# Expert phase of a fused decoder layer: gate products spread, weights loaded in chained pieces, feature transposes behind the weighted sums

## The chip, the cores and the metric

One core of a Trainium2 chip runs one program. The metric is the time of one launch on the device in microseconds (us), as the median over several runs. The profile comes from one further execution.

## The reference, cut to what matters

The input is 4096 tokens (2 sequences of 2048) of 512 features; a decoder layer of three parts is computed in float32, each with a residual.

```
x = x + gated_recurrence(layernorm(x))
x = x + cross_attention(layernorm(x), ctx) @ Wo + bo       # 16 heads, 77 keys
xf = layernorm(x)
scores = xf @ gate_W + gate_b                              # 4 experts
top2, weights = top_k(scores, 2), softmax(top2 scores)
expert e: layernorm(relu(layernorm(xf @ W1[e] + b1[e]) * g1[e] + be1[e]) @ W2[e] + b2[e]) * g2[e] + be2[e]
x = x + xf + sum over the two experts of weight * expert(xf)
```

With the reference's own inputs the first 2048 tokens send 697, 1052, 1151 and 1196 rows to experts 0 to 3.

## The kernel before, in words

**Precision.** A float32 product is made of three products of a high and a low part (TERMS). ScalarE (ACT) writes the high part of an operand, VectorE (DVE) then writes what is left as the low part; TensorE (PE) takes high*high, high*low, low*high.

**Phase A and B.** Eight chunks of 512 tokens pass the recurrence (A) and then the attention (B). A turn of B interleaves the attention of chunk c with the output projection, the third layernorm, the feature transposes and the gate scores of chunk c-1, in an order written out by hand for each engine. `t_bank` and `mm_bank` are two PSUM banks each; the lists `T_LAST`, `MM_LAST`, `TAIL` and their like (L320 to L324) say in which order groups take them, alternating, and a group waits (`t_free`, `mm_free`) until the group before it in its bank is read. `last_turn` (PE L1023, ACT L1422, DVE L2176, POOL L2537) is the turn of the last chunk, 7. The projection of chunk 7 (`project`, L885) follows it: four groups of 12 products of 128x512.

**Gate.** `gate_products` (L903) has, for a tile of 128 tokens, 4 products with a moving side of only 4 columns; `gate_scores` writes a chunk's 16 pairs of weight load and product (32 instructions in the trace, where each float32 product counts as two). In turns of the loop they stand tile by tile between other products; in the last turn all of chunk 6's stand together (L1060), and chunk 7's stand together in the first expert tile (L1154).

**Expert phase (C).** Sorted rows are worked on in 67 tiles of 128 rows, each with one expert. The first 29 are planned from the first four chunks: full tiles in the order of the experts, so with the counts above tiles 0 to 4 are expert 0's, 5 to 12 expert 1's, 13 to 20 expert 2's, 21 to 28 expert 3's. `c_tile` is the body of a tile i on every engine. PE (L1144): transposes the hidden rows of tile i, transposes the gathered rows of tile i+3 (`rows_in`), first product of tile i+2 (12 products), second product of tile i (12 products). POOL (L2587): inverse roots (`rstd`), the gather of the rows of tile i+5, one scatter into the slot table, then `add_out`, which adds the rows of tile i-1 into the output by an indirect DMA; it waits until the add of the tile before has landed (L2573), and the next `rstd` is queued behind it. DVE has the statistics, low parts, and between them the routing of the last chunk and the plan of the other 38 tiles (`route_between`, `route_behind`).

**SP** issues the other DMAs in program order (L614 to L664). `load_expert(s)` brings half s of the eight expert halves (s = 2e+w, for W1 or W2 of expert e) as one DMA of 2 MB; `expert_in(s)` waits for it and raises `experts_ready`, in the order of s; halves 0, 4 and 1 are loaded during the last attention turn. The first product with expert e waits for 2e+1, the second for 2e+2 (L1113, L1130). `load_slots` brings the 128 rows of the slot table of one tile (1 KB), after the load of the tile two before has landed; `gather_rows` on DVE waits for it five tiles ahead. All these DMAs and the stores are in one queue.

```
            for s in range(5, 2 * NE):
                load_expert(s)
                load_slot_pairs(2 * s - 1, min(2 * s + 1, EARLY // 2))
                expert_in(s)
```

## Time and profile before

| | us |
|---|---|
| median of 3 timed runs | 1216.72 (1214.84 to 1219.3) |
| the profiled execution, its own time | 1209.59 |
| its span in the profile | 1207.8 |
| PE busy | 1159.6 (96%) |
| DVE, ACT, POOL busy | 924.9, 731.5, 457.2 |

"Busy" sums an engine's instructions. "Idle before" in a timeline stands in brackets, with what ended it. PEclk is the granted clock of TensorE as a share of full speed: 1.00 is 2.4 GHz, 0.50 is 1.2 GHz. In the timelines a start differs from the next start by the time that really passed; the durations of neighbouring matmul groups overlap a little.

### The profile page before, as it was taken

What the parts mean: (1) busy time and instruction counts of PE and PEld (TensorE: products, weight loads), DVE (VectorE), ACT (ScalarE), POOL (GpSimd) and SP (SyncE); (2) the same over time, 40 slices, a digit from 0 to 9 for tenths busy, and PEclk for the clock granted to TensorE, in tenths of its full rate; (3) what the DMA queues carried; (4) which work ended last, traced back from release to release, by engine and by line L of the source; (5) the groups of instructions that cost most, each with busy time, mean ns of one, the idle gap of its engine ahead of it and who ended that gap; (6) DMA issues with size and microseconds to landing.
All of it is one profiled execution on the core that took longest, in us unless ns stands there. A gap on an engine that the chain in (4) does not pass through costs nothing.

```text
span 1207.8 us, 24523 instructions
## 1 busy us (share of the span) xinstructions
PE 1159.6 (96%) x6041; PEld 978.9 (81%) x6042; DVE 924.9 (77%) x2196; ACT 731.5 (61%) x2114; POOL 457.2 (38%) x410
## 2 busy tenths in 40 slices
PE   6999999999989999999999998989999999999993
PEld 5788888888878888888888877867888888888882
DVE  6888888887766677877868777678777777777774
ACT  5323333233486757767677662567777777777773
POOL 4040000000052314535445164357655555555543
PEclk9999999999999999999999998899999999999998
DMA  8754544444520302133021358885554444444433
GB/s 271 230 160 160 188 176 146 174 156 165 199 84 1 105 10 97 44 107 104 10 97 44 131 131 227 270 221 122 81 88 81 85 79 86 80 85 80 85 64 42
DMA packets 83237, 143.90 MB, mean 119 GB/s; under 512 B 20460, under 2 KB 24752, under 8 KB 82309
## 3 DMA queue, kind: packets, MB, share of 16 engines
q1 hardware_dynamic: 63872, 101.60, 25.8%
q0 software_dynamic: 18464, 39.14, 17.1%
q10 hardware_dynamic: 837, 2.41, 0.6%
q8 instruction: 28, 0.46, 0.2%
q14 instruction: 36, 0.29, 0.1%
HBM read 78.83 MB, written 67.83 MB: 121 GB/s over the span
## 4 chain that ended last, share of the span: by engine, by line
PE 83%; DMA 5%; DVE 4%; issue 3%; ACT 3%; POOL 2%; POOLq 0%; DVEq 0%; SPq 0%; ACTq 0%
PE banks L1097 27%; PE banks L681 21%; PE banks L746 7%; PE banks L891 6%; PE banks L879 5%; DMA out<-rows,scatter_rows 4%; PE banks L848 3%; PE banks L865 3%; PE banks L1109 2%; PE banks L907 2%; PE banks L1125 2%; ACT rows L1310 2%; PE banks L719 1%; PE banks L800 1%; PE banks L765 1%
## 5 line engine op out<-in xcount | busy, mean ns | idle before, releaser
L1097 PE MATMUL banks<-operands 128*128 x1608 | 388.6, 396 | 10.5 <-DVE operands L1570 5.2
L1097 PEld LDWEIGHTS banks<-operands 128*128 128x128 f32 x1608 | 298.1, 189 | 73.6 <-issue 7.4
L681 PE MATMUL banks<-operands 128*128 128x512 f32 (+2 forms) x1224 | 292.6, 394 | 3.5 <-DVE operands L1570 3.5
L681 PEld LDWEIGHTS banks<-operands 128*128 128x128 f32 (+1 forms) x1224 | 225.6, 192 | 47.8 <-DVE operands L1570 3.7
L1570 DVE TENSOR_TENSOR operands<-banks,operands 128x512 fp32r<-128x512 f32 (+3 forms) x328 | 217.7, 682 | 42.5 <-ACT operands L1189 38.8
L1189 ACT ACTIVATE operands<-banks 128x512 fp32r<-128x512 f32 (+3 forms) x328 | 191.7, 608 | 96.7 <-PE banks L879 45.0
L1310 ACT ACTIVATE rows<-banks,score_shift 128x77 f32<-128x77 f32 x512 | 162.7, 374 | 28.0 <-DVE score_shift L1792 27.2
L1189 ACT ACTIVATE operands<-rows 128x512 fp32r<-128x512 f32 (+3 forms) x79 | 55.3, 709 | 163.8 <-DVE rows L1641 138.1
L1495 ACT ACTIVATE banks<-banks,param_cols 128x128 f32<-128x128 f32 x268 | 99.2, 430 | 82.5 <-PE banks L1125 82.5
L2576 POOL DMA_INDIRECT out<-rows,scatter_rows x67 | 106.6, 1591 | 104.2 <-DVE rows L2315 65.1
L1310 ACT ACTIVATION_READ_ACCUMULATOR rows<-banks,score_shift 128x1 f32 x512 | 129.1, 256 | 0.0
L2500 POOL TENSOR_TENSOR rows<-rows,score_rec 128x1232 f32<-128x1232 f32 x32 | 72.1, 2253 | 147.3 <-DVE score_rec L1800 147.3
L2262 DVE BATCH_NORM_STATS2 moe_stats<-banks 128x6 f32<-128x512 f32 x134 | 93.2, 695 | 43.9 <-PE banks L1097 42.5
L891 PE MATMUL banks<-operands 128*128 128x512 f32 x384 | 97.7, 406 | 0.0
L746 PE MATMUL banks<-operands 128*128 128x512 f32 x384 | 91.6, 394 | 0.1
L2585 POOL TENSOR_TENSOR moe_rstd<-moe_var_eps,minus_half 128x2 f32<-128x2 f32 (+1 forms) x70 | 52.4, 748 | 83.8 <-DVE moe_var_eps L2275 83.8
L746 PEld LDWEIGHTS banks<-operands 128*128 128x128 f32 x384 | 70.9, 188 | 15.7 <-DVE operands L1570 1.3
L891 PEld LDWEIGHTS banks<-operands 128*128 128x128 f32 x384 | 72.0, 194 | 14.2
L2557 POOL DMA_INDIRECT rows<-xf_rows,gather_rows x67 | 69.3, 1034 | 30.8 <-issue 24.9
L879 PE MATMUL banks<-operands 103*128 103x512 f32 (+1 forms) x288 | 75.6, 403 | 2.0 <-DVE operands L1783 1.4
L2460 POOL TENSOR_TENSOR ln_rstd<-ln_var_eps,minus_half 128x4 f32 (+1 forms) x8 | 10.1, 1262 | 170.8 <-DVE ln_var_eps L1665 170.8
L2513 POOL DMA_INDIRECT slot_table<-slot_payload,slot_rows x64 | 65.1, 1018 | 19.8 <-issue 13.7
(178 smaller groups left out, 1707.0 us busy)
## 6 DMA issues: line engine op xcount, KB each, us to landing
expert_parts<-operands SPq DMA_DIRECT2D x32, 512.0 KB, 3.0
operands<-expert_parts SPq DMA_DIRECT2D x8, 2048.0 KB, 11.1
rows<-in_x SPq DMA_DIRECT2D x8, 1024.0 KB, 5.4
rows<-in_L_ffn_W SPq DMA_DIRECT2D x32, 256.0 KB, 3.5
x_rows<-rows SPq DMA_DIRECT2D x8, 1024.0 KB, 4.3
rows<-x_rows SPq DMA_DIRECT2D x8, 1024.0 KB, 5.7
xf_rows<-rows SPq DMA_DIRECT2D x32, 256.0 KB, 2.7
out<-rows SPq DMA_DIRECT2D x32, 256.0 KB, 2.5
```

The costliest lines, as they stand in the source:

```text
L681: last = nc.tensor.matmul(dst, stationary(a, k), moving(b, k), start=(t == 0 and k == 0), stop=(t == len(terms) - 1 and k == n_k - 1))
L746: last = nc.tensor.matmul(g_bank[m % 2], wg[:, a, k, m * P:(m + 1) * P], hTr[:, a2, k, :], start=(k == 0 and t == 0), stop=(k == KC - 1 an ...
L879: last = nc.tensor.matmul(mb(c, f"v{m}"), vblk[0:n, a, m, u, :], pT[0:n, a2, u, :], start=(t == 0 and u == 0), stop=(t == len(TERMS) - 1 a ...
L891: last = nc.tensor.matmul(mb(at, f"o{j}"), out_part(c, a, m)[:, j * P:(j + 1) * P], wo[:, a2, m, :], start=(m == 0 and t == 0), stop=(m == ...
L1097: last = nc.tensor.matmul(dst, stationary[:, a, k, :], weights[:, w, bass.ds(e, 1), a2, k, :].rearrange("p e f -> p (e f)"), start=False, ...
L1189: return nc.scalar.activation(dst, src, ACT.Copy, scale=scale)
L1310: nc.scalar.activation(pb[m % 2][:, j, keys], s_banks[:, j, keys], ACT.Exp, bias=nmax[:, m % 2, at], scale=-1.0, accum_out=ssum[:, m % 2, ...
L1495: nc.scalar.activation(ch_bank[:, at], ch_bank[:, at], ACT.Relu, scale=pcol[:, bass.ds(e * KC + (ROW_G1 + k), 1)], bias=pcol[:, bass.ds(e ...
L1570: return V.tensor_tensor(dst, src, hi.bitcast(F32), ALU.subtract)
L2262: V.bn_stats(c_st[:, which, :], src).then_inc(stat, 1)
L2500: G.tensor_tensor(p3, p3, srec[:, m % 2, :].unsqueeze(2).to_broadcast([P, TPC * HPG, SK]), ALU.mult).then_inc(p_ready, 1)
L2576: G.indirect_dma_start(out, bass.IndirectOffsetOnAxis(six[u][:, 0:1], 0), y2[u], None, compute_op=ALU.add).then_inc(added[u], 16)
```

## The change

- PE, last turn: the transposes of feature tile 1 of chunk 6 move behind the weighted sums (`attend`) of heads 2, those of tile 2 behind the sums of heads 3. DVE: `plan_early(1)` moves behind `read_positions`; `out_lo` of heads 2 and 3 and the low parts stand ahead of feature copies.
- Gates of chunk 6: tile 0 at the end of the last turn, tile 1 and tiles 2, 3 between halves of the first projection group. Gates of chunk 7: out of tile 0 into tile 1, tiles 0 and 1 inside the first product of expert tile 3, tiles 2 and 3 inside the second product of expert tile 1; the position products go into tile 2. The routing and planning steps of DVE move one tile later.
- SP: `load_expert(3)` is taken from between the stores and issued right behind `load_expert(2)`, and four slot pairs follow; halves 5, 6 and 7 are loaded in 16 pieces of 64 rows (128 KB), each issued when the one before has landed, with a slot pair behind each eight.
- POOL: four scatters of chunk 5 move ahead of `ln3_pow(7, 0)`. PE and ACT read the first three tiles' experts at once.
- Banks: `m1_bank`, `m2_bank` are (6, 7), (3, 1); gates and positions of chunk 7 use the two row banks (4, 5).
- ACT: the load of be2 and its waits move behind the hidden norm of tile 1, `fill_first(1, ...)` ahead of the base rows.

```diff
@@ -590,8 +592,18 @@
+            PIECES = 4 * KC
+
+            def load_expert_parts(s, parts):
+
+                e, w = s // 2, s % 2
+                for n in parts:
+                    a, k, rows = n // (2 * KC), n // 2 % KC, slice(n % 2 * (P // 2), (n % 2 + 1) * (P // 2))
+                    need(sp, w_in[s], 16 * n)
+                    sp.dma_start(weights[rows, w, e, a, k, :].bitcast(F32), ws_d[s, a, k, rows]).then_inc(w_in[s], 16)
+
             def expert_in(s):
-                sp.wait_ge(w_in[s], 16)
+                sp.wait_ge(w_in[s], 16 if s < 5 else 16 * PIECES)
...
@@ -633,24 +645,25 @@
             for j in range(2):
                 store_base(last - 1, j, slot3(last - 1)[:, j, :])
             load_slot_pairs(3, 5)
-            load_expert(3)
             for j in range(2, TPC):
                 store_base(last - 1, j, slot3(last - 1)[:, j, :])
+            expert_in(1)
             sp.wait_ge(mm_done, mm_num(NCH, "o3") + 1)
             for j in range(TPC):
                 store_xf(last, j)
             for i in range(2):
                 sp.wait_ge(base_out[i], 16 * 2 * last)
             load_rows(g2_rows, "L0_ffn_g2", g2_in)
-            expert_in(1)
-            load_slot_pairs(5, 7)
             load_expert(2)
-            load_slot_pairs(7, 9)
+            load_expert(3)
+            load_slot_pairs(5, 9)
             for s in range(2, 5):
                 expert_in(s)
             for s in range(5, 2 * NE):
-                load_expert(s)
-                load_slot_pairs(2 * s - 1, min(2 * s + 1, EARLY // 2))
+                for half_n in range(2):
+                    pair = 2 * s - 1 + half_n
+                    load_expert_parts(s, range(PIECES // 2 * half_n, PIECES // 2 * (half_n + 1)))
+                    load_slot_pairs(pair, min(pair + 1, EARLY // 2))
                 expert_in(s)
             for j in range(TPC):
...
                 project(c - 1, c, 3)
                 probs_to_keys(c, 2, (2,))
                 xf_to_features(c - 1, c, 0)
+                attend(c, 2)
                 xf_to_features(c - 1, c, 1)
-                attend(c, 2)
 
                 probs_to_keys(c, 3, (0, 1))
                 pe.wait_ge(s_read, TPC * HPG * KC * NCH)
                 rows_in(0, 0)
                 probs_to_keys(c, 3, (2,))
+                attend(c, 3)
+
                 xf_to_features(c - 1, c, 2)
-                attend(c, 3)
-
                 xf_to_features(c - 1, c, 3)
                 pe.wait_ge(experts_ready, 1)
-                prime(m1_bank[0])
+                for bank in m1_bank:
+                    prime(bank)
                 rows_in(0, 1)
-                gate_scores(c)
+                gate_scores(tail, (0,))
...
+                    between()
                 pe.wait_ge(cx_lo, i + 1)
                 expert_product(m1_bank[u], e, 0, xT, (2,)).then_inc(m1_done, 1)
...
                 if between is not None:
-                    hidden_in(*between)
+                    between()
                 expert_product(m2_bank[u], e, 1, hTc, (2,)).then_inc(m2_done, 1)
...
                 early = i if isinstance(i, int) else FRONT
+                if early == 0:
+                    pe.wait_ge(mm_read, mm_num(tail, "o3") + 1)
                 if after >= 2:
                     hidden_in(i, u)
-                if after >= 3:
+                if early == 0:
+                    pe.wait_ge(mm_read, mm_num(tail, "r") + 1)
+                    prime(m2_bank[0])
+                if early == 2:
+                    pe.wait_ge(tail_gate_read, 1)
+                if early == 3:
+                    pe.wait_ge(tail_pos_read, 1)
+                if after >= 3 and early >= 1:
                     rows_in(n + 1 + u, 1 - u)
-                if early == 0:
-                    pe.wait_ge(b_t_read, t_num(tail, "xf3") + 1)
-                    prime(m2_bank[0])
-                    gate_products(tail_bank, tail, range(TPC)).then_inc(tail_gate_done, 1)
-                if early == 1:
-                    pe.wait_ge(tail_pos_read, 1)
-                    prime(m2_bank[1])
                 experts = coming()
                 if after >= 2:
-                    first_product(i + 2, u, experts[4])
-                second_product(i, u, experts[2], (i + 1, 1 - u) if 1 <= after < 3 else None)
+                    first_product(i + 2, u, experts[4], prime_and_gates if early == 1 else
+                                  last_positions if early == 2 else None)
+                second_product(i, u, experts[2], last_gates if early == 1 else
+                               (lambda: hidden_in(i + 1, 1 - u)) if 1 <= after < 3 else None)
                 if early == 0:
-                    pe.wait_ge(tail_gate_read, 1)
-                    pe.wait_ge(route, NROUTE * last + ROUTE_COUNTED)
-                    position_products(tail_bank, True).then_inc(tail_pos_done, 1)
-
-            last, tail = NCH - 1, NCH
+                    rows_in(1, 1)
+
+            def prime_and_gates():
+
+                pe.wait_ge(b_t_read, t_num(tail, "xf3") + 1)
+                prime(m2_bank[1])
+                pe.wait_ge(cx_lo, 4)
+                gate_products(tail_g_bank, tail, range(2))
+
+            def last_gates():
+                gate_products(tail_g_bank, tail, range(2, TPC)).then_inc(tail_gate_done, 1)
+
+            def last_positions():
+
+                pe.wait_ge(route, NROUTE * last_of_b + ROUTE_COUNTED)
+                pe.wait_ge(cx_lo, 5)
+                position_products(tail_r_bank, True).then_inc(tail_pos_done, 1)
             last_turn(last)
-            for j in range(TPC):
+            project(last, tail, 0, (0, 1))
+            gate_scores(tail, (1,))
+            project(last, tail, 0, (2, 3))
+            pe.wait_ge(plan_ready, 1)
+            first_experts = [expert_at(pe, i) for i in range(3)]
+            gate_scores(tail, (2, 3))
+            for j in range(1, TPC):
                 project(last, tail, j)
             positions(last - 1, tail, "r")
-            pe.wait_ge(plan_ready, 1)
-            first_product(0, 0, expert_at(pe, 0))
+            first_product(0, 0, first_experts[0])
             for j in range(2):
                 xf_to_features(last, tail, j)
-            pe.wait_ge(mm_read, mm_num(tail, "o3") + 1)
-            prime(m1_bank[1])
-            first_product(1, 1, expert_at(pe, 1))
+            first_product(1, 1, first_experts[1])
+            rows_in(1, 0)
             for j in range(2, TPC):
                 xf_to_features(last, tail, j)
-            rows_in(1, 0)
-            pe.wait_ge(mm_read, mm_num(tail, "r") + 1)
-            tiles_of(pe, c_tile)
+            tiles_of(pe, c_tile, first_experts)
...
+                if early == 2:
+                    route_weights(NCH - 1)
+                if early >= 2:
+                    weighed_be2(*((n, 0) if u else (n - 1, 1)), experts[1])
+                if after >= 1:
+                    hidden_norm(i + 1, 1 - u)
...
+                if early == 1:
+                    act.wait_ge(be2_in, 16)
+                    act.wait_ge(b_t_read, t_num(NCH, "xf3") + 1)
+                    weighed_be2(0, 0, experts[1])
...
+            fill_first(0, 0, first_experts[0])
+            act.wait_ge(primed, 2)
+            fill_first(1, 1, first_experts[1])
             for j in range(2, TPC):
                 base_in_place(NCH - 2, j)
+            route_weights(NCH - 2)
             for j in range(2):
                 base_in_place(NCH - 1, j)
             rows_hi(1, 1)
-            act.wait_ge(primed, 2)
...
             def last_turn(c):
                 pT_lo_part(c, 0, (0, 1))
                 max_scores(c, 1, 1)
-                plan_early(1)
                 x2_rows(c - 1, c, 0)
                 pT_lo_part(c, 0, (2,))
                 count(c - 2)
@@ -2185,6 +2228,7 @@
                 max_scores(c, 2, 0)
                 ln3_pair(c - 1, 0)
                 read_positions(c)
+                plan_early(1)
                 plan_early(2)
 
                 max_scores(c, 2, 1)
@@ -2207,23 +2251,21 @@
                 x2_rows(c - 1, c, 3)
                 xf_features(c - 1, c, 0)
                 ln3_pair(c - 1, 1)
+                out_lo(c, 2)
...
                 xf_features(c - 1, c, 1)
-                out_lo(c, 2)
 
                 pT_lo_part(c, 3, (0, 1))
+                rows_lo(0, 0)
+                pT_lo_part(c, 3, (2,))
                 ln3_apply(c - 1, c, 2)
                 ln3_apply(c - 1, c, 3)
-                pT_lo_part(c, 3, (2,))
+                out_lo(c, 3)
                 xf_features(c - 1, c, 2)
-                rows_lo(0, 0)
-                out_lo(c, 3)
                 xf_features(c - 1, c, 3)
                 for i in range(2):
                     gather_rows(1, i)
                 weigh(c - 2)
                 slots(c - 2, c, aside=1)
-                gate_bias(c)
-                choose(c - 1, c)
 
             q_lo(0, 0)
...
                 hidden_lo(i)
-                if early == 0:
+                if early == 1:
                     dve.wait_ge(tail_gate_done, 1)
-                    biased_scores(tail_bank).then_inc(tail_gate_read, 1)
+                    biased_scores(tail_g_bank).then_inc(tail_gate_read, 1)
...
                     statistics(i + 2, 0, m1_bank[u], m1_done, c1_stat)
                     moments(i + 2, 0, c1_stat, c1_aggr)
+                if early == 0:
+                    for j in range(2, TPC):
+                        xf_features(NCH - 1, NCH, j)
+                    coming()
                 if after >= 3:
                     rows_lo(i + 3, 1 - u)
+                if early == 0:
+                    plan_early(3)
...
+            gate_bias(tail)
+            choose(last - 1, tail)
             count(last - 1)
             x2_rows(last, tail, 1)
             ln3_pair(last, 0)
...
@@ -2605,11 +2655,9 @@
 
             last = NCH - 1
             gather(1, 0)
-            for j in range(2):
+            for j in range(TPC):
                 scatter(last - 2, j, aside=1)
             ln3_pow(last, 0)
-            for j in range(2, TPC):
-                scatter(last - 2, j, aside=1)
             gather(1, 1)
             ln3_pow(last, 1)
             rstd(-1, True, False)

```

## Rows read from the trace of the kernel before

**Rows 1.** The page's part 4, the chain that ended last, by engine and by line

```profile
PE 83%; DMA 5%; DVE 4%; issue 3%; ACT 3%; POOL 2%; POOLq 0%; DVEq 0%; SPq 0%; ACTq 0%
```

**Rows 2.** PE timeline, 722 to 767 us: start, us, instructions [idle before <-releaser]

```profile
722.37 4.11 PE L907 MATMUL banks<-gate_w,rows 128*128 128x4 f32 x32
726.34 13.92 PE L891 MATMUL banks<-operands 128*128 128x512 f32 x48
...
746.39 3.01 PE L1097 MATMUL banks<-operands 128*128 x12 [1.50 <-ACT banks L1483]
...
753.53 0.66 PE L1109 MATMUL banks<-ident,rows 128*128 128x128 f32 x4 [2.39 <-DMA rows<-xf_rows,gather_rows]
...
754.26 5.15 PE L907 MATMUL banks<-gate_w,rows 128*128 128x4 f32 x32
759.27 7.40 PE L1097 MATMUL banks<-operands 128*128 x24
```

**Rows 3.** Windows, PE alone: stretch, length, busy (instructions), granted clock, DMA share, GB/s

```profile
640.00:705.00 65.00, 63.35 (x370) 1.00 0.23 82
756.00:763.00 7.00, 7.00 (x26) 0.51 1.03 385
819.00:1180.00 361.00, 360.94 (x1815) 1.00 0.47 83
```

**Rows 4.** PE timeline of one turn of phase B before: one tile's gate products

```profile
681.70 0.95 PE L907 MATMUL banks<-gate_w,rows 128*128 128x4 f32 x8
```

**Rows 5.** PE timeline, waits of the last attention turn

```profile
712.64 0.66 PE L899 MATMUL banks<-ident,rows 128*128 128x128 f32 x4 [0.95 <-DVE operands L1570]
...
718.70 0.63 PE L899 MATMUL banks<-ident,rows 128*128 128x128 f32 x4 [0.64 <-DVE rows L1842]
```

**Rows 6.** PE timeline, starts of expert tiles 3 and 8 and products between them

```profile
780.62 0.60 PE L1125 MATMUL banks<-ident,rows 128*128 128x128 f32 x4
...
781.41 4.79 PE L1097 MATMUL banks<-operands 128*128 x20
788.18 1.20 PE L1097 MATMUL banks<-operands 128*128 x4 [1.98 <-DVE operands L1570]
...
803.51 1.79 PE L1097 MATMUL banks<-operands 128*128 x4 [2.29 <-DVE operands L1570]
...
820.07 0.60 PE L1125 MATMUL banks<-ident,rows 128*128 128x128 f32 x4
```

**Rows 7.** POOL timeline: an add that waited, and the inverse roots behind it

```profile
799.80 1.60 POOL L2576 DMA_INDIRECT out<-rows,scatter_rows  x1 [4.28 <-DMA out<-rows,scatter_rows]
800.84 1.33 POOL L2585 TENSOR_TENSOR moe_rstd<-moe_var_eps,minus_half 128x2 f32<-128x2 f32 x1
```

**Rows 8.** SP timeline: loads of g2, of halves 2 and 5, and two slot loads

```profile
756.23 0.34 SPq L598 DMA_DIRECT2D rows<-in_L_ffn_g  x1
765.02 0.43 SPq L590 DMA_DIRECT2D operands<-expert_parts  x1
...
775.03 0.34 SPq L606 DMA_DIRECT2D rows<-slot_table  x1
775.65 0.40 SPq L590 DMA_DIRECT2D operands<-expert_parts  x1
...
778.41 0.34 SPq L606 DMA_DIRECT2D rows<-slot_table  x1
```

**Rows 9.** Time to landing: stores after 780 us; quiet reads of 256 KB, 1 MB

```profile
out<-rows SPq DMA_DIRECT2D x4, 256.0 KB, 2.6
...
DMA to landing us min/median/max: 2.5/2.7/4.3
...
DMA to landing us min/median/max: 5.4/5.4/5.6
```

**Rows 10.** PE timeline, expert tile 21: its 24 products between the heads of tiles

```profile
903.70 5.71 PE L1097 MATMUL banks<-operands 128*128 x24
909.25 0.60 PE L1125 MATMUL banks<-ident,rows 128*128 128x128 f32 x4
```

More of the change, by code:

```diff
@@ L914, in gate_scores @@
                     mm_free(at, "g")
-                last = gate_products(mb(at, "g"), at, tiles)
+                last = gate_products(mb(at, "g"), last_of_b if isinstance(at, int) and at == tail else at, tiles)
                 if tiles[-1] == TPC - 1:
@@ L2406, in _ @@
             norm_shift(0)
[L2407 to L2408 removed]
+            rows_lo(2, 0)
             statistics(1, 0, m1_bank[1], m1_done, c1_stat)
```

86 lines of the change are left out of this document (41 added, 45 removed).

## The prediction, made before the changed kernel was run

> **What bounds the kernel now.** I read the chain of waits first: PE has 83% of it [rows 1]. Then the windows: from 819 to 1180 us PE is busy for 360.94 of 361 us [rows 3]. So nothing that the change does to another engine in that stretch can help, and every microsecond by which PE reaches 819 earlier moves the end by as much, as long as its weights are there. The same row gives the cost of an expert tile: 32 instructions (24 products, 8 transposes) of 361/1815 us, 6.36 us. The losses that can be had lie between 700 and 820 us, and the PE timeline shows three kinds.
>
> First, the clock. Chunk 6's gates are 32 narrow instructions in 4.11 us, and the 48 projection products behind them take 13.92 us [rows 2], where 24 like products take 5.71 us at full clock [rows 10], so 48 would take 11.4. Chunk 7's 32 take 5.15 us and the 24 products behind them 7.40 [rows 2]; the window over both has a granted clock of 0.51, the lower level, 1.2 GHz [rows 3]. In the turns of phase B the gates of a tile are 8 instructions (0.95 us) between other work [rows 4], and from 640 to 705 us the clock is 1.00 [rows 3].
>
> Second, waits of PE on the way into the expert phase: 1.50 us for ACT and 2.39 us for a gather [rows 2], 0.95 and 0.64 us for feature tiles in the last turn [rows 5].
>
> Third, the expert tiles 3 to 7: from 780.62 to 820.07 they take 39.45 us where five tiles are 31.8. In them PE waits 1.98 and 2.29 us for low parts [rows 6]. Behind those stands POOL: an add waited 4.28 us for the add before it, and the inverse roots of the next tile stood behind it [rows 7]. In that stretch three 2 MB loads of expert halves run, the first from 775.65 [rows 8].
>
> **The change, part by part.** *Gates spread.* The same 64 narrow instructions stay, so what can be won is the slow clock: 13.92 - 11.4 = 2.5 us, 5.15 - 4.11 = 1.0 us, 7.40 - 5.71 = 1.7 us, together 5.2 us. Bounds: nothing, if sixteen narrow ones in a row still lower the clock (chunk 6's tiles 2 and 3, both halves of chunk 7), and 5.2. I take 5.2, since the nearest row is the group of eight in a loop with full clock.
>
> *Transposes behind the weighted sums, gather and fills earlier.* The waits of 0.95, 0.64, 1.50 and 2.39 us go, 5.5 us. The gather of tile 3 has no 2 MB load next to it and is read by PE one tile later, so the 2.39 has cover. New waits, estimated from the order: the third group of transposes of heads 3 needs the bank of feature tile 1, which DVE now reads behind `out_lo` (1.2 us); the first product of tile 1 still waits for ACT, which has two base rows in front of its high part (0.6, of 1.5 now); three value loads in a row behind six projection products (0.5); the position products of chunk 7 wait in tile 2 for DVE's count, which now stands behind low parts (1.0). That is 3.3, bounds 1 to 6. Net 2.2 us. `plan_early(1)` behind `read_positions` only swaps small DVE steps; four scatters ahead of an inverse root on POOL have the cover of the projection. I cost both at nothing; without that cover it would be some 0.3 us. The primes are moved, not added.
>
> *Weight pieces.* With one piece of 128 KB in flight instead of a 2 MB load, adds need not queue with it: the 39.45 - 31.8 = 7.65 us of tiles 3 to 7 go. Bounds: half of it, if the adds are late for other reasons, and all. I take all, because from 819 on, with adds and gathers alone, no such wait is left [rows 3].
>
> *Halves 2 and 3 together.* The g2 load, at 756.23 now [rows 8], waits for base stores that stand behind the 2 MB load of half 3; without that load I put it at 747. Behind it come some 7.5 MB (g2, two halves, be2, stores, gathers). At the 385 GB/s of [rows 3] they end near 766.5. Slot pairs 5 to 8 stand behind them in the same queue, and each waits for the pair before: one such round was at most 3.38 us (775.03 to 778.41) [rows 8], so three rounds end at 774 to 776. Only then does SP tell PE of half 2. PE wants it for the first product of tile 5, at 781.41 now [rows 6], minus the 7.4 us won so far: 774.0. I take 1 us lost, bounds 0 and 6.
>
> *The chain of 48 pieces.* A quiet read of 256 KB lands in 2.5 us and one of 1 MB in 5.4 [rows 9]; the line through them gives 2.0 us for 128 KB. In the expert phase a 256 KB store took 2.6 us [rows 9]; for half the size I add 0.35 us of contention: 2.35 us a piece (bounds 2.0, and the 3.38 of a slot load). Each of the five slot pairs between pieces adds about 0.8 us to the chain, since its two issues take longer than a piece is in flight. The chain then needs 48 x 2.35 + 4 + 1 = 117.8 us from its start. PE has, from the first product of tile 5 to the second product of tile 21 (expert 3's first, needing half 7), 781.41 to 906.6 (the middle of [rows 10]) = 125.2 us, less the 7.65: 117.5 us. So the last half arrives as PE asks for it. In a margin of nothing every error on one side costs, so I take 2 us.
>
> By the Trainium skill, "DMA: Bandwidth & Descriptors", section "Bandwidth", and the fixed cost before it, a transfer takes about 2.0 us plus its bytes at 436 GB/s, and DMAs should be batched to 1 MiB or more. By that a piece is 2.3 us and the chain 115.4 us, just in time, where one 2 MB load would be 6.8 us; this is the rule that speaks against the pieces. No row here shows a piece of 128 KB.
>
> **Sum.** 5.2 + 2.2 + 7.65 - 1 - 2 = 12.0 us off the profiled execution's own 1209.59 us: 1197.6. The median of the timed runs is 1216.7, 7 us above that execution; the same step gives 1204.7 for the median. A measurement of this kernel can tell about 0.5%, 6.1 us, from no change.
>
> **Rivals.** *The pieces come too late* (this one ends slower). Place: `experts_ready` in front of the second product of tile 21. Each 0.1 us on a piece costs 4.8 us. The gain is used up when a piece takes 2.65 us, and it is a loss over 0.5% from 2.78; at 3.1 us the wait is 36 us and the time about 1238. For it: the slot loads' 3.38 us with hardly any bytes, and gathers and adds of 256 KB in every tile (DMA share 0.47 [rows 3]). Against it: a slot load is 128 tiny elements, a piece is 64 rows of 2 KB, and the measured reads and stores are near 2.5 for twice the bytes. Between 2.53 and 2.78 us the result is within 0.5%. I give 0.14 to slower, 0.14 to this middle.
>
> *The clock still falls* behind sixteen narrow instructions, since neighbours of 16 are twice the 8 of [rows 4] and, in the first tail, only six products part the groups. Then 5.2 is lost again: 1209.9, still faster. 0.14.
>
> *Half 2 late.* If the two loads move at less than 385 GB/s, or the three slot rounds need 3.4 us each, PE waits 6 us in front of tile 5 instead of 1, perhaps with a slow clock behind it: 1210. 0.10.
>
> *The adds still bind*: POOL's own work per tile plus an add's landing is the limit whatever SP loads, so that half of the 7.65 stays: 1208.5. Against it stands the unbroken stretch after 819. 0.06. That the change doesn't do what it says, because the weights were never in the adds' way, is part of this.
>
> **How the numbers follow.** The forecast with its own range, 1199 to 1209, has 0.42. Faster by over 0.5% (below 1210.6): forecast 0.42, the clock 0.14, and half of the next two 0.08: 0.64. Within 0.5%: the middle of the pieces 0.14 and the other half 0.08: 0.22. Slower: 0.14. The range goes from 1199 (all waits gone, pieces early) to 1221, a piece at 2.75 us; less than 2 in 10 lies outside.
>
> **What would show it.** In the profile after: a granted clock of 1.00 around the projection of chunk 7 and in expert tile 1 (gates), with the 42 later projection products near 10 us; no bracket for a gather at the row transposes of tile 3; expert tiles 3 to 8 at 6.4 us each with adds landing in about 5 us; the SP timeline with pieces 2.3 to 2.5 us apart; PE's first wait behind tile 2 in front of tile 5's first product, 0 to 3 us; and in front of tile 21's second product a wait near zero. A wait there of over 14 us, or pieces over 2.65 us apart, would make the forecast wrong in sign; a clock of 0.5 in either gate stretch makes it wrong in size.

## The result, and the profile after

The kernel after takes 1249.72 us (median of 4 runs, 1248.66 to 1255.96), the kernel before beside it 1217.97 (4 runs, 1214.84 to 1219.3): a ratio of 1.0275 on record, 95% interval 1.0235 to 1.0315 (the two medians alone give 1.026). It is slower by 2.75%, where the forecast was 1204.7 us, range 1199 to 1221. What came true is the rival "the pieces come too late". Two later executions far above the others of their kernel, one of the kernel before (1304.92 us) and one of e10_rows_first (1666.95 us), are left out of all medians and ratios.

The profiled execution took 1249.72 us (span 1247.9). Its page, part 4 (the chain that ended last, by engine and by line) and the costliest group of part 5:

```profile
PE 64%; DMA 13%; issue 8%; DVE 5%; ACT 4%; SPq 3%; POOL 1%; DVEq 0%; ACTq 0%; POOLq 0%
...
L1115 PE MATMUL banks<-operands 128*128 x1608 | 393.7, 400 | 46.4 <-SPq L607 37.8
```

PE had 83% of the chain before [rows 1] and has 64% now. The expert products (L1115) waited 46.4 us in all, 37.8 of them for SP's line 607, the increment of `experts_ready`. The waits of PE from 700 to 960 us, grouped (us in total, times, longest):

```profile
PE banks L1115 <- SPq L607: 37.8, 2, 25.1
PE banks L1115 <- DVE operands L1614: 4.4, 2, 2.2
PE banks L938 <- DVE rows L1861: 4.0, 1, 4.0
PE banks L892 <- ACT operands L1229: 1.6, 3, 0.8
PE banks L878 <- DVE rows L1891: 0.9, 1, 0.9
```

and their places in the PE timeline (start, us, instructions, in brackets the idle time before and its releaser):

```profile
782.03 1.19 PE L1115 MATMUL banks<-operands 128*128 x4 [2.23 <-DVE operands L1614]
...
880.24 1.20 PE L1115 MATMUL banks<-operands 128*128 x4 [2.19 <-DVE operands L1614]
...
901.40 8.39 PE L1115 MATMUL banks<-operands 128*128 x24 [12.71 <-SPq L607]
...
944.89 4.47 PE L1115 MATMUL banks<-operands 128*128 x12 [25.12 <-SPq L607]
```

The last two are nearly the whole loss. At 901.40 the first product of tile 21 had waited 12.71 us for half 6, at 944.89 the second product of the same tile 25.12 us for half 7. Behind each wait PE runs at the lower clock for a while: 24 products in 8.39 us instead of 5.71 [rows 10], 12 in 4.47 instead of half of that, 2.86. That is 4.3 us more. The late low part at 880.24 (2.19) is a debt of the chain too: DVE had waited 4.46 us, until 878.55, for a row of the slot table, and SP issued that load at 876.47, behind 24 pieces. So the bill of the weights is 12.71 + 25.12 + 2.19 + 4.3 = 44.3 us.

SP's queue shows why. Start, us and number of piece issues (L603) in one stretch beside gathers and adds, and in one where PE waits:

```profile
782.84 15.50 SPq L603 DMA_DIRECT2D operands<-expert_parts  x5
...
925.85 16.91 SPq L603 DMA_DIRECT2D operands<-expert_parts  x7
```

The last piece is issued at 942.29. So 48 pieces, slot pairs included, took 944.8 - 782.84 = 162 us, 3.37 us each, where the prediction had 117.8. By the issue times of the single pieces, which a narrower window shows one by one, the first 24 gaps are 3.97 us on average, the last 12, mostly while PE waits and POOL with it, 2.68; the shortest are 2.4 to 2.5.

The other parts of the change, in the windows of PE (stretch, length, busy time and instructions, granted clock, DMA share, GB/s):

```profile
724.00:741.00 17.00, 15.22 (x86) 1.00 0.96 215
762.00:773.00 11.00, 10.56 (x66) 1.00 1.04 386
783.00:874.00 91.00, 90.95 (x460) 1.00 0.67 118
901.00:948.00 47.00, 21.47 (x83) 0.68 0.40 97
```

Both gate stretches now run at full clock, where the second had 0.51 [rows 3]. Between 783 and 874 us PE is busy throughout, where tiles 3 to 7 lost 7.65 us before [rows 6]: the adds are no longer late.

What each part was worth shows when the expert phase is split at the first transposes of expert tile 3 (780.62 us before, 783.06 after). From there to the last row transposes the kernel before takes 389.4 us and the kernel after 426.9. The kernel after with 256 KB pieces and nothing else altered (e3 below) takes 382.8, which is 44.1 us less: the bill of 44.3 closes. Ahead of tile 3, from the position products of the last turn on, the kernel after takes 89.0 us where the kernel before took 87.3. The gates, worth some 6.4 us there (e7 below), are more than used up. PE's waits in this part rose from 7.4 to 11.1 us in all, the longest of them 3.99 us in front of L938 and 2.23 us in front of 782.03, and the low clock behind the first cost 2.5 us (the next 12 products took 5.47 us, not 3.0). These terms add up to 0.2 us less than before where 1.6 more were measured, so about 2 us of this part are not accounted for.

### The profile page after: what moved, and what is told of

Read it like the earlier page. It is cut to its first block, busy times and chain, and to the rows that moved or that the text cites. A ratio compares the mean times of both kernels' runs of the same rounds, so it can differ in the third digit from the quotient of the medians.

```text
span 1247.9 us, 24559 instructions
## 1 busy us (share of the span) xinstructions
PE 1161.1 (93%) x6041; PEld 977.8 (78%) x6042; DVE 925.7 (74%) x2196; ACT 731.7 (59%) x2114; POOL 455.2 (36%) x410
## 4 chain that ended last, share of the span: by engine, by line
PE 64%; DMA 13%; issue 8%; DVE 5%; ACT 4%; SPq 3%; POOL 1%; DVEq 0%; ACTq 0%; POOLq 0%
PE banks L1115 19%; PE banks L694 16%; DMA operands<-expert_parts 8%; PE banks L759 6%; PE banks L905 4%; PE banks L892 4%; DMA rows<-slot_table 3%; PE banks L861 3%; PE banks L878 3%; ACT rows L1350 2%; PE banks L1145 2%; PE banks L1127 1%; PE banks L922 1%; ACT operands L1229 1%; DVE operands L1614 1%
## 5 line engine op out<-in xcount | busy, mean ns | idle before, releaser
L1115 PE MATMUL banks<-operands 128*128 x1608 | 393.7, 400 | 46.4 <-SPq L607 37.8
L1115 PEld LDWEIGHTS banks<-operands 128*128 128x128 f32 x1608 | 300.6, 191 | 110.7 <-issue 45.1
L861 PE MATMUL banks<-operands 128*128 128x308 f32 (+1 forms) x384 | 71.4, 310 | 0.0
```

What stands on the lines that cost most here:

```text
L861: last = nc.tensor.matmul(s_banks[:, j, :], qT[:, a, m, j * P:(j + 1) * P], keys, start=(t == 0), stop=(t == len(TERMS) - 1 and j > 0))
L1115: last = nc.tensor.matmul(dst, stationary[:, a, k, :], weights[:, w, bass.ds(e, 1), a2, k, :].rearrange("p e f -> p (e f)"), start=False, ...
```

## The experiments

Times are compared with runs of the kernel before on the same chip (its medians: 1210.5 for the first four, 1212.88 for the pair of gates and turn, 1213.1 and 1212.05 for the last ones). Since the granted clock also differs between runs of the same code (last section), I read each profile over a fixed stretch as well: from the position products of the last attention turn to the last row transposes of the expert phase. Both ends are rows of the PE timeline, such as `693.30` and `1170.05` us for the kernel before: 476.8 us. The last two columns split it at the first transposes of expert tile 3. The part behind tile 3 repeats well: 382.3 to 383.5 us in five profiles with small enough pieces. The part ahead of it does not: the same code of this part took 83.1, 83.1, 83.9, 83.2, 83.6, 86.6 and 89.0 us (e1, e3, e4, e5, e6, e9, after), and the code of the kernel before 87.3, 85.7 and 85.8 (before, e2, e11). There is one profile of each kernel, so differences of 1 to 2 us ahead of tile 3 show nothing. The ratios are those on record; the quotients of the medians differ from them by up to 0.2 percentage points.

| kernel | median (runs) | ratio to before, 95% | stretch, us | to tile 3 | behind |
|---|---|---|---|---|---|
| before | | | 476.8 | 87.3 | 389.4 |
| after | 1249.72 (4) | 1.0275 [1.0235, 1.0315] | 515.9 | 89.0 | 426.9 |
| e1_whole | 1212.47 (10) | 1.0012 [0.9993, 1.0031] | 474.6 | 83.1 | 391.5 |
| e2_only_pieces | 1244.18 (4) | 1.0262 [1.0243, 1.028] | 507.3 | 85.7 | 421.6 |
| e3_256k | 1203.02 (4) | 0.9925 [0.9907, 0.9943] | 465.9 | 83.1 | 382.8 |
| e4_two_flight | 1204.73 (4) | 0.9942 [0.9922, 0.9961] | 466.7 | 83.9 | 382.9 |
| e5_few_adds | 1242.68 (1) | | 504.1 | 83.2 | 421.0 |
| e6_few_gathers | 1241.16 (1) | | 502.9 | 83.6 | 419.3 |
| e7_gates | 1208.88 (9) | 0.9969 [0.9945, 0.9992] | 475.1 | 85.5 | 389.6 |
| e8_turn | 1208.57 (10) | 0.9958 [0.9936, 0.9979] | 473.1 | 84.0 | 389.1 |
| e9_tell_early | 1207.01 (10) | 0.9949 [0.9922, 0.9976] | 469.8 | 86.6 | 383.2 |
| e10_rows_first | 1203.16 (8) | 0.9922 [0.9894, 0.995] | 466.4 | 82.9 | 383.5 |
| e11_before_256k | 1203.52 (5) | 0.9939 [0.991, 0.9969] | 468.1 | 85.8 | 382.3 |
| e12_pieces_512k | 1200.7 (4) | 0.9911 [0.988, 0.9943] | 466.8 | 81.4 | 385.4 |

**The change with 2 MB loads again (e1_whole).**

```diff
-                for half_n in range(2):
-                    pair = 2 * s - 1 + half_n
-                    load_expert_parts(s, range(PIECES // 2 * half_n, PIECES // 2 * (half_n + 1)))
-                    load_slot_pairs(pair, min(pair + 1, EARLY // 2))
+                load_expert(s)
+                load_slot_pairs(2 * s - 1, min(2 * s + 1, EARLY // 2))
```

> The changed kernel with halves 5, 6 and 7 loaded whole (2 MB) again, all else as changed. Theory A (the chain of pieces is the whole loss: 12.7 + 25.1 + 2.2 us of waits and 4.3 us at the low clock behind them, and whole loads do little harm): 1249.7 - 44.3 = 1205.4, no wait of PE for the experts. Theory B (whole loads bring back the late adds of the kernel before): some 7.6 us more, 1213, with PE waits for low parts in expert tiles 3 to 8.

Measured 1212.47 us, no different from before: theory B. The waits for halves 6 and 7 are gone, and the collisions are back. PE timeline, and below it POOL's adds (L2624) in the same profile:

```profile
805.76 1.97 PE L1113 MATMUL banks<-operands 128*128 x4 [1.96 <-DVE operands L1612]
...
822.95 2.08 PE L1113 MATMUL banks<-operands 128*128 x4 [2.58 <-DVE operands L1612]
```

```profile
802.04 1.62 POOL L2624 DMA_INDIRECT out<-rows,scatter_rows  x1 [3.90 <-DVE gather_rows L2321]
...
819.08 1.62 POOL L2624 DMA_INDIRECT out<-rows,scatter_rows  x1 [5.96 <-DMA out<-rows,scatter_rows]
```

An add that waits 3.90 or 5.96 us makes the inverse root behind it late, and PE's low part with it, as in [rows 6, 7].

**The pieces alone (e2_only_pieces).** The kernel before with `load_expert_parts` and its loop, nothing else.

> The kernel before with only the chained pieces of 128 KB. Theory A: the chain takes about 162 us as in the changed kernel, from about 776 on, so the last half arrives near 938 where PE wants it at 899 to 907; the time is 1218 + 32 to 39 and 4 for the low clock, 1250 to 1258. Theory B' (the chain is slow only because of other edits): under 1225.

Measured 1.0262: nearly the whole loss of the change. The median is 33.7 us above that of the kernel before beside it, where theory A had 32 to 40. Its waits in the PE timeline:

```profile
896.59 7.83 PE L1109 MATMUL banks<-operands 128*128 x24 [8.78 <-SPq L605]
941.23 4.95 PE L1109 MATMUL banks<-operands 128*128 x12 [26.84 <-SPq L605]
```

**The same chain with 256 KB a piece (e3_256k).**

```diff
-            PIECES = 4 * KC
+            PIECES = 2 * KC
...
-                    a, k, rows = n // (2 * KC), n // 2 % KC, slice(n % 2 * (P // 2), (n % 2 + 1) * (P // 2))
+                    a, k = n // KC, n % KC
                     need(sp, w_in[s], 16 * n)
-                    sp.dma_start(weights[rows, w, e, a, k, :].bitcast(F32), ws_d[s, a, k, rows]).then_inc(w_in[s], 16)
+                    sp.dma_start(weights[:, w, e, a, k, :].bitcast(F32), ws_d[s, a, k]).then_inc(w_in[s], 16)
```

> The changed kernel with 8 pieces of 256 KB (128 rows of 2 KB) a half in place of 16 of 128 KB, still one in flight. If a piece costs mostly a fixed time plus waiting behind the gathers and adds, a piece takes 3.0 us quiet and near 4 us beside them, the chain under 100 us, no PE wait for experts, 1206. If a piece's time grows with its bytes (what is left of the DMA engines is the limit), 6.7 us a piece and 1249 as now.

Measured 1203.02 us, faster than before by 0.75%. DMA issues between 785 and 878 us (count, KB each, median us to landing), and the only waits of PE from 784 to 1190 us:

```profile
operands<-expert_parts SPq DMA_DIRECT2D x24, 256.0 KB, 3.8
out<-rows,scatter_rows POOLq DMA_INDIRECT x15, 5.5
```

```profile
PE banks L1115 <- ACT operands L1229: 3.6, 3, 1.8
```

The 24 pieces are issued 3.94 us apart, the last at 875.79, and PE never waits for an expert. A piece of twice the bytes costs what one of 128 KB costs in the same company (3.97), so half the number takes half the time. Other profiles show how exact this is: the first 24 gaps of e2's 128 KB pieces are 3.74 us on average, and 256 KB pieces are 3.74 to 4.01 us apart in e7 to e11.

**Two 128 KB pieces in flight (e4_two_flight).** Even and odd pieces are chained each on its own semaphore.

```diff
-                    need(sp, w_in[s], 16 * n)
-                    sp.dma_start(weights[rows, w, e, a, k, :].bitcast(F32), ws_d[s, a, k, rows]).then_inc(w_in[s], 16)
+                    odd = n % 2
+                    landed = w_in[s - 5 if odd else s]
+                    need(sp, landed, 16 * (n // 2 + odd))
+                    sp.dma_start(weights[rows, w, e, a, k, :].bitcast(F32), ws_d[s, a, k, rows]).then_inc(landed, 16)
```

> The changed kernel with 16 pieces of 128 KB a half, but two in flight (even and odd pieces are chained apart). Fixed-time theory: the chain halves to 80 to 90 us, no PE wait for experts, 1206. Limit-by-bytes theory: 1249 as now.

Measured 1204.73 us. A piece lands in 4.1 us (median), two at a time, and the 48 take some 98 us (80 to 90 were expected). So the size of 128 KB is not at fault by itself; what was short is bytes per round trip.

**Who makes a round trip 3.97 us long? (e5_few_adds, e6_few_gathers.)** In the kernel after, e5 adds only the first 16 of the 128 rows of tiles 0 to 16, and e6 gathers only 16 of the 128 rows of tiles 5 to 22; the rest of those rows is left out.

```diff
+                few = 16 if isinstance(i, int) and i < FRONT else P
-                G.indirect_dma_start(out, bass.IndirectOffsetOnAxis(six[u][:, 0:1], 0), y2[u], None,
+                G.indirect_dma_start(out, bass.IndirectOffsetOnAxis(six[u][0:few, 0:1], 0), y2[u][0:few], None,
```

> The changed kernel, with the adds of tiles 0 to 16 reduced to 16 of their 128 rows each (the other rows of these tiles are not added to the output). If a piece of 128 KB is slow because it stands beside the adds, the pieces in the stretch from 785 to 870 us come 2.5 to 3.0 us apart instead of 3.7 to 4.0, and PE's two waits for experts shrink from 37.8 us together to under 20. If the adds are not the cause, the spacing stays at 3.7 or more and so do the waits.

> The changed kernel, with the gathers of tiles 5 to 22 reduced to 16 of their 128 rows each (the rest of the row tile keeps older rows). If the gathers are what the pieces stand beside, spacing 2.5 to 3.0 us; if the adds are, it changes by less than a fifth from 3.7 to 4.0; if both alike, 3.1 to 3.4 in this run and in the one with small adds.

The first 24 gaps fall from 3.97 us to 3.35 with few adds and to 3.45 with few gathers; the last 12 stay at 2.78 and 2.76. The quiet gap is 2.45, so adds account for 0.62 and gathers for 0.52 of the 1.5 us above it, and neither alone is the cause. That is close to the third of the cases named; 3.35 lies between the two cases that the first run had, and 3.45 just outside the third. PE's waits for halves 6 and 7 are 6.25 and 27.21 us with few adds and 4.63 and 25.89 with few gathers, 33.5 and 30.5 in all, not under 20. Each is one execution and one profile, and e2's 3.74 shows how far such a mean can move by itself.

The packet records of the same traces (queue q1, between one piece's issue and the next) show what the 1.5 us are. In the ten shortest gaps of the kernel after, under 2.5 us, the first packet of a piece starts 1.27 us after its issue, its 64 packets take 0.70 us from the first start to the last end, and the next piece goes out 0.48 us later. In the first 24 gaps these are 1.68, 1.74 and 0.56 us. So two thirds of the added time pass while the piece's own packets move, among those of gathers and adds, and 0.4 us before its first packet. With few adds the middle term is 1.31 us. A 256 KB piece of e3 has 1.38, 2.19 and 0.38 us.

**Gates together again, on the 256 KB version (e7_gates).** `gate_scores(tail)` in one call ahead of the projection, and all four tiles of chunk 7 in expert tile 1.

> The changed kernel with 256 KB pieces, and with each chunk's gate products together again: chunk 6's 32 instructions in front of the last projection, chunk 7's 32 inside the first product of expert tile 3. If spreading them is what keeps the clock up, the granted clock falls to 0.50 behind each group, the 48 projection products take 13.9 us again and not about 11.5, and the time is 4 to 5 us above that of the kernel with 256 KB pieces (1207 to 1208 where that has 1203). If the clock fell for another reason, same time as that kernel, 1203.

Measured 1208.88 us, 0.44 percentage points over the 256 KB version. PE timeline of e7, then of the version with the gates spread (e3_256k):

```profile
728.02 4.35 PE L922 MATMUL banks<-gate_w,rows 128*128 128x4 f32 x32
732.23 13.68 PE L905 MATMUL banks<-operands 128*128 128x512 f32 x48
...
766.00 4.74 PE L922 MATMUL banks<-gate_w,rows 128*128 128x4 f32 x32
770.60 6.01 PE L1115 MATMUL banks<-operands 128*128 x16
```

```profile
734.08 1.84 PE L922 MATMUL banks<-gate_w,rows 128*128 128x4 f32 x16
735.78 8.41 PE L905 MATMUL banks<-operands 128*128 128x512 f32 x36
...
765.13 1.84 PE L922 MATMUL banks<-gate_w,rows 128*128 128x4 f32 x16
766.84 3.03 PE L1115 MATMUL banks<-operands 128*128 x12
```

From the first gate to the position products it is 745.75 - 728.02 = 17.7 us together and 744.03 - 729.50 = 14.5 spread. From the fill of `m2_bank[1]` (L1161) to the hidden transposes of tile 2 it is 776.45 - 765.77 = 10.7 and 772.43 - 764.91 = 7.5. So the spreading is worth 3.2 + 3.2 = 6.4 us in these two places. The granted clock is the one expected; windows of PE behind the second group in e7, and around it in e3:

```profile
770.00:774.00 4.00, 4.00 (x12) 0.50 1.04 361
```

```profile
765.00:772.00 7.00, 7.00 (x49) 1.00 1.03 367
```

Against that, e7 has no wait of 2.2 us in tile 2, and no low clock behind it; ahead of tile 3 it is only 2.4 us longer than e3. And it has something else, in front of tile 5's first product, which with its low clock is most of the 6.8 us that e7 loses behind the head of tile 3. So the median's 0.44 points are not the price of the gates alone:

```profile
789.28 3.90 PE L1115 MATMUL banks<-operands 128*128 x10 [4.75 <-SPq L607]
```

**The last turn in its old order (e8_turn).** PE's and DVE's transposes and low parts as before, on the 256 KB version.

> The changed kernel with 256 KB pieces, and with the last attention turn's order as before: feature transposes 1 and 2 in front of the weighted sums, DVE's low parts, feature copies and planning steps in their old places. The waits of 0.95 and 0.64 us come back and the ones of 0.94 and 0.88 go: theory A (the new order only swaps waits) the same within 1 us, 1203. Theory B (the order is worth what its old waits said): 1.5 to 2 us slower, 1205.

Measured 1208.57 us, 0.33 percentage points over the 256 KB version, with intervals that just overlap. The waits in the turn change places rather than go: 0.95 and 0.64 us for feature tiles in the old order, as in [rows 5], 0.94 and 0.83 in the kernel after. The wait for half 2 is there again, 5.07 us, and the 24 products behind it take 7.41 us, not 5.71. Without these 6.8 us the stretch would be 466.3, 0.4 above the 256 KB version's: the turn's order is worth less than one profile can tell, as theory A said.

**Half 2 told early (e9_tell_early).** Over the profiles of e1, e3 to e8 and the kernel after, PE's wait for half 2 in front of tile 5 is 0 (twice), 0.47, 0.64, 1.26, 2.19, 4.75 and 5.07 us.

```diff
-            load_slot_pairs(5, 9)
+            load_slot_pairs(5, 6)
             for s in range(2, 5):
                 expert_in(s)
+            load_slot_pairs(6, 9)
```

> Edit on the kernel with 256 KB pieces (1203.0 us): SP tells PE of halves 2, 3 and 4 behind the first slot pair instead of behind four of them. Theory A (half 2 has long landed when SP says so, since SP waits for slot rounds that queue behind the two 2 MB loads): no wait of PE for experts in front of tile 5's first product in any profile, where profiles of like kernels show 0 to 5 us; the median 0 to 3 us below that kernel's, 1200 to 1203. Theory B (the 2 MB load of half 2 itself lands late): the wait stays at 0 to 5 us and the time at 1203. The chain of pieces should start where it did, near 785 us.

Neither this profile nor the two of the later kernels that keep the edit has the wait. The time, 1207.0, is not below e3's 1203.0; but e3's own profile has no such wait, and the intervals of the two ratios overlap. In e3, e7 and e8 half 2 had landed at 770.48, 774.09 and 771.59 us, and SP told of it at 784.90, 789.12 and 786.77, 14 to 15 us later. So theory A's mechanism is shown; what it is worth in the median is not measured. SP's queue in e3 shows how slot loads come to hold up the news of half 2:

```profile
755.18 0.94 SPq L592 DMA_DIRECT2D operands<-expert_parts  x1
756.89 9.21 SPq L618 DMA_DIRECT2D rows<-slot_table  x1
777.98 1.44 SPq L618 DMA_DIRECT2D rows<-slot_table  x2
```

The slot load behind the two 2 MB loads took 9.21 us to be issued, and the next pair, which waits until it has landed, went out at 777.98, 21 us after it. Half 2 was told behind three more such rounds.

**Output rows ahead of the gates (e10_rows_first).** In e3, DVE idles for 4.91 us in expert tile 1 for chunk 7's gates, with `out_rows` of tile 0 standing behind them. POOL's add of tile 0 waited 9.53 us for it, and the inverse root of tile 2 stands behind that add.

```diff
                 if early == 1:
+                    out_rows(*last)
                     dve.wait_ge(tail_gate_done, 1)
...
                     count(NCH - 1)
-                    out_rows(*last)
```

> On top of the edit before: in expert tile 1 DVE computes the output rows of tile 0 ahead of its wait for chunk 7's gates, in which it idled 4.9 us, instead of behind the counts. POOL's add of tile 0 then goes out near 770 instead of 777.9 us and no longer stands in front of the inverse root of tile 2. Theory A (the wait of 2.2 us for a low part in tile 2 comes from that order, and the clock level of 0.5 behind it from the wait): that wait falls below 0.7 us and the products behind it run at full clock, 2 to 3.5 us less than the edit before. Theory B (the low part waits for DVE's own work on the gates, whatever the order): the wait falls by 0.8 us at most, and the time by under 1 us.

PE timeline of e9, and of e10:

```profile
779.62 2.08 PE L1116 MATMUL banks<-operands 128*128 x4 [2.20 <-DVE operands L1615]
781.50 1.05 PE L1146 MATMUL banks<-ident,rows 128*128 128x128 f32 x4
```

```profile
782.36 1.19 PE L1116 MATMUL banks<-operands 128*128 x4 [0.32 <-issue]
783.39 0.60 PE L1146 MATMUL banks<-ident,rows 128*128 128x128 f32 x4
```

The wait falls from 2.20 to 0.32 us and the products behind it keep the full clock (1.19 instead of 2.08 us, transposes 0.60 instead of 1.05). That is theory A in its mechanism. The stretch is 3.5 us shorter than e9's and the median 3.9 us, but e9 is itself 3.9 us longer than e3, from which it differs only in the order of SP's slot loads. Against e3 neither the stretch (466.4 and 465.9) nor the median (1203.16 and 1203.02) is shorter. So what the edit is worth in time is not shown.

**The kernel before with 256 KB pieces alone (e11_before_256k).**

> The kernel before with halves 5 to 7 in chained pieces of 256 KB and nothing else of the change. Theory A (what the pieces give is the adds that no longer queue behind 2 MB loads, 7.6 us by the waits of tiles 3 to 8, and 24 pieces of 4 us are early enough): 4 to 8 us below the kernel before, 1204 to 1209 us here, no wait for experts at tile 21, and the other part of the change then gives the 3 us that are left to the version with 256 KB pieces. Theory B (the gates and the turn give most of it): within 2 us of the kernel before, 1209 to 1212.

Measured 0.9939 [0.991, 0.9969], 1203.52 us, and a stretch 8.6 us shorter than before: theory A. Of these 7.1 us lie behind the head of tile 3, where the pieces can act; the other 1.5 lie in code that is the same. It is within the error of e3, so all else in the change together adds 2.2 us by the stretch (468.1 to 465.9), and nothing that the medians can tell. The gates give 6.4, and the wait and low clock of tile 2 and the moved waits of the turn take most of it back.

**512 KB a piece (e12_pieces_512k),** on e10: `PIECES = KC`, two values of `k` in one transfer.

> The last version (output rows ahead of the gates, 256 KB pieces) with 12 pieces of 512 KB, one in flight, instead of 24 of 256 KB. Theory A (a piece costs what the traffic beside it costs, nearly whatever its size, and the adds wait longer the larger a piece is): 4.5 to 6 us a piece, the chain over near 845 us; adds of tiles 5 to 12 wait 2 to 4 us for the add before them, where with 256 KB they wait 1.5 to 1.7; PE then waits for a low part in none to two of these tiles, 0 to 3 us, and the time is 0 to 4 us above the version with 256 KB (1205.4). Theory B (only loads of 2 MB are in the adds' way): the adds wait no longer than with 256 KB, and the time is the same within 1 us.

Twelve pieces, 781.73 to 843.64, 5.6 us apart. Adds wait up to 2.51 us for the add before them, in e10 up to 2.35 in the same stretch; PE waits for low parts four times, 0.23 to 0.68 us, 1.7 us in all:

```profile
826.12 1.21 PE L1117 MATMUL banks<-operands 128*128 x4 [0.68 <-DVE operands L1616]
833.16 1.19 PE L1117 MATMUL banks<-operands 128*128 x4 [0.39 <-DVE operands L1616]
```

The price of a piece is theory A's; the adds wait hardly longer than with 256 KB, which is theory B's. Behind the head of tile 3 the kernel takes 385.4 us, e10 383.5: 1.9 us more, about the waits for low parts. The whole stretch hides it (466.8 and 466.4), since the code ahead of tile 3, the same in both, took 1.5 us less. The median, 1200.7, is the lowest measured here, 0.9% below before, but its ratio is not to be told from e10's.

## Why the prediction was wrong

*What bounds the kernel, and where the losses lie*: right. PE ran without a gap from 783 to 874 us, and each wait before 820 us moved the end by its own length.

*Gates spread, 5.2 us*: right for the gates themselves. Groups of 16 keep the clock at 1.00; undone, they cost 6.4 us (e7). But most of it was lost again to the wait in tile 2 (next point).

*The last turn, 2.2 us*: the mechanism was right in that new waits take the place of old ones, the size was wrong. Ahead of tile 3 the forecast had 7.4 us off, gates and turn together. The kernel after takes 1.6 us more than the kernel before; the same code in e3 takes 4.2 us less, e4 to e6 3.5 to 4.2. With the gates at 6.4, the turn and the first tiles lost 2 to 3 us in those and 8 in the kernel after, where 2.2 were to be won. Of the new waits that I listed, the positions in tile 2 came as 0.42 us instead of 1.0. One was missing from the list: DVE's wait for the gates in tile 1 has the output rows of tile 0 queued behind it, behind those stand POOL's add and the inverse root of tile 2, and behind that PE's low part (2.2 us; in e3 and e9 a lower clock behind it). The prediction doesn't name the move of `out_rows` behind the counts, and so costed it at nothing. In the profile of the kernel after, a further 3.99 us in front of the position products came from a late DVE step (`L1861`, idle 4.24 us); the other profiles with the same code there have 0 to 1 us. I did not find its cause; it stays open.

*Adds no longer late, 7.65 us*: right. e1 brings the waits back; e11 has this gain alone and takes 7.1 us less behind the head of tile 3.

*Halves 2 and 3 together, 1 us, bounds 0 to 6*: inside the bounds, with 0 to 5 us in the profiles, but by luck. The bulk was through at 776 to 778 us, not at 766.5, and the slot rounds took some 2.2 us, not 3.38, so in the kernel after SP told PE at 782.5, 7 us later than forecast. PE asked at 783.85, and not at 774.0, and so waited for nothing.

*The chain of 48 pieces, 2 us*: this is the step that failed. I priced a piece at 2.35 us: 2.0 from a line through two quiet reads [rows 9], and 0.35 for contention. Quiet pieces do take 2.4 to 2.5 from start to start, so the line itself was 0.4 short for a chained piece, whose successor must also see it land. Part of this is a misread row: 2.5 us for a quiet read of 256 KB is the shortest of eight, the median is 2.7 [rows 9], and with it the line gives 2.25. Beside the gathers and adds the mean was 3.97 for half of the chain, 1.5 us of contention in place of 0.35. Over 48 pieces, slot pairs included, 3.37 us: 162 us instead of 117.8, with 117.5 to be had. The upper bound that I named myself, the 3.38 us of a slot load, was close to the true price; that it met the mean to 0.01 us is luck, since the mean is one of a slow first half and a quicker second. I set it aside because such a load has 128 tiny elements; but e3 shows that in this traffic 128 and 256 KB cost the same, so the slowest small transfer in the same stretch was the nearest row, and the quiet reads the far one. The four stores of 2.6 us [rows 9], my check of it, were issued within 1.5 us, at 815 to 817 us, and took 2.2 to 4.6. Single gaps of the busy half are 2.4 to 5.3 us, so one such moment was no measure of the stretch.

With the whole chain at its measured length the rival's rule gives the result: 162 - 117.8 = 44.2 us on a chain with no margin, 1204.7 - 2 + 44.2 = 1246.9, against 1249.72. That it comes so near owes something to the start from the median: from the profiled execution's own 1209.59 us the same working gives 1239.8, and the 10 us between that and 1249.72 are in the main the gains ahead of tile 3 that did not come. I also watched half 7 alone, at the second product of tile 21; half 6 was late as well, by 12.71 us.

By the Trainium skill, "DMA: Bandwidth & Descriptors", section "Anatomy of one DMA", the fit of 2.0 us and the bytes at 436 GB/s, measured there on DMAs that GpSimd issues, gives an estimate of 2.3 us a piece. The quiet stretches of SP's pieces agree within 0.2 us; the first half of the chain, 3.97, does not, and the fit says nothing of other traffic. The same page, section "Queues, rings and completion order", says that each DMA engine goes round its queues and drains a whole packet of one before it turns to the next. The packets of a piece that spread from 0.70 to 1.74 us beside gathers and adds, and the shares that e5 and e6 take away, agree with that; in which order one DMA engine took them was not read. The page's section "Bandwidth" advises batches of 1 MiB or more. Against 128 KB with one in flight that was right, and here it was too strong: 256 and 512 KB were enough, and 2 MB loses some 7 us to late adds. No run has pieces of 1 MB.

## What to carry to other kernels

A chain of transfers with one in flight is a round trip per piece: take its price from the slowest small transfer in the same stretch and the same company, not from a quiet one (here 3.4 us, where the quiet reads gave 2.0), multiply by the count, and compare with the time at which each half is asked for. If large loads get in the way of latency-bound transfers, choose the piece so that the chain has a wide margin (here 256 KB, landed at 878 us where half 7 is asked for near 903), or keep two in flight. And for each wait moved onto an engine, walk the queue behind it to the bound engine: here DVE, POOL, DVE, PE.

## What the runs showed of the hardware

*Price of a chained piece beside gathers and adds of 256 KB each*: 128 KB 3.7 to 4.0 us (e2, after), 256 KB 3.7 to 4.0 (e3, e7 to e11), 512 KB 5.6 (e12); quiet, 128 KB 2.4 to 2.5, of which 1.27 pass before the first packet, 0.70 while the packets move and 0.48 behind them. Two 128 KB pieces in flight land in 4.1 us each (e4).

*A small load behind two of 2 MB in one queue*: 9.21 us to be issued, 21 us until the load that waits for it goes out (e3).

*The clock differs ahead of the change.* In code that all kernels share, the position products of the last turn start between 692.91 us (e12) and 700.50 (e10). Windows of PE in e10 and in e9:

```profile
680.00:690.00 10.00, 9.38 (x56) 0.83 0.68 238
```

```profile
680.00:690.00 10.00, 9.38 (x62) 1.00 0.84 315
```

Even with groups of eight gate products the clock sometimes falls: in e10 six products of the weighted sums behind such a group took 2.91 us where e9's took 1.64. Runs of one kernel differ by some 10 us (e10: 1199.54 to 1209.01, at granted clocks of 0.996 and 0.989), more than most single steps here are worth; that the clock ahead of the change makes all of this difference is not shown. So small steps were read from a stretch that begins behind that point, and the smallest from its part behind tile 3.
